# Six stages on one core: the scan's norm statistics and first front issued inside the routed stage, the second expert stage's first router front issued inside attention

## The chip, the cores and the metric

One core of one Trainium2 chip. The time is the device time of one execution in microseconds (us), the median of several runs. The core's engines work side by side from queues of their own: TensorE (PE; its weight loads are shown as PEld), VectorE (DVE), ScalarE (ACT), GpSimd (POOL), and SyncE (SP), which here issues the DMAs. Each engine takes its instructions in the order in which they are written; semaphores hold an instruction until another engine has come far enough.

## The reference

The input is 8 sequences of 512 tokens with 128 features, fp32. Six layers follow, each on a layer norm of x and added to x:

```
x = x + 0.5 * ffn0(norm(x))      # top 2 of 8 experts (128x128), softmax of the two scores
x = x + attn0(norm(x))           # attention on cos and sin features of q and k, one head
x = x + 0.5 * ffn0(norm(x))
x = x + 0.5 * ffn1(norm(x))      # 16 experts mix q, k, v and the output; causal attention
x = x + attn1(norm(x))           # selective scan: 256 channels x 16 states, convolution of 4 taps
x = x + 0.5 * ffn1(norm(x))
```

In `attn1` the normed x gives a convolved and gated u, a step dt (softplus), B and C (16 rows each) and a gate. The recurrence is `h = exp(dt*A)*h + dt*u*B`; its products with C are summed over the 16 states, `u*D` is added, the gate is applied, and a matmul leads back to 128 features.

## The kernel before

x stays in SBUF as `xs` for the whole program. The six layers run as six stages in a row, and after each stage four engines meet in a barrier (`layer_end`: drain, then a wait for all four). SyncE takes no part in it. Inside a stage the work is ordered by a clock written out by hand: each engine steps through the same slots u, issues its unit of that slot, and then the steps that `due` finds for it. A step belongs to a generator (`front(b)` prepares a sequence, `back(b)` finishes it), and a tuple of slots beside its start says when each of its pieces is issued. An engine may run ahead of the others as far as its semaphores let it.

**Expert stages (layers 0 and 2, `ffn`).** Two groups of four sequences. `front(G)` is the router of one group: VectorE's statistics of 16 tiles (L1313) and seven small operations, GpSimd's power (L566), the norm's bias on VectorE (L1328), 16 normalised tiles on ScalarE (L676), transposes on PE into bank 0 (L901), ScalarE's copies (L682), scores on PE (L909, eight matmuls a sequence), the top two on VectorE (L1331 to L1356), one exponential on ScalarE, a transpose (L933), a copy (L703). SyncE writes these rows to DRAM and reads each back over all partitions (L504, L509). Then VectorE makes one product per sequence and expert (L1397), 64 in all, and PE eight matmuls for each (L960). The front of group 0 runs before the first product; that of group 1 in the slots of group 0.

**Attention (layer 1).** Eight turns, one sequence each. `front(b+1)` (norm, q, k, v, features) is interleaved with `main(b)` (four blocks of scores, L991, exponentials, L737, weighted sum, L1000, residual on VectorE, L1433). VectorE issues norm, normalised tile and features of the next sequence, and then waits for the weighted sum. GpSimd makes only the norm's power (L571).

**Routed stages (layers 3 and 5, `routed`).** Slots of 24 a sequence: 16 expert products (L1517) with eight matmuls each for q, k and v (L1103), then 8 products for pairs of experts (L1106) that belong to the sequence before. `back(b)` is the causal attention of sequence b (L1045 to L1063 on PE, maxima L1487 on VectorE, L775 and L780 on ScalarE). The last sequence's attention has 16 slots without units around it (u = 192 to 207); its pairs come at 208 to 215, its residual (L1496) at 218.

**Scan (layer 4).** 32 slots a sequence, one of (16 states x 2 halves) each. ScalarE makes the decay (L861), GpSimd the products with B (L603) and, for five states, with C (L612); VectorE runs the recurrence (L1574) and the other products with C (L1566); PE sums over the states (L1218) and spreads C (L1206). `front(b)` makes everything that sequence b needs: on VectorE the statistics (L1260 to L1272), the bias (L1527), u (L1533), dt (L1541), gate (L1545); on ScalarE the normalised tiles (L807), copies, tanh, abs, exp and ln with three table loads; on PE transposes (L1148), convolution (L1157), the matmul for delta, B and C (L1168), two remainders (L1175), z (L1182), res (L1186). Its slots start 16 before the sequence that runs before it, so sequence 0's front stands ahead of the first recurrence, and so do the first pieces of sequence 1's. B and C go through DRAM (`bc_to_dram`, `widen_B`, `widen_C` on SyncE). The ring of products with B is six deep, that of products with C eight.

The lines that set the scan's order on VectorE before:

```
steps = on_clock(front, (-16, -14, -3, 6, 13, 16, 18, 20), back, (4, 5, 10))
for U in SCAN_CLOCK:
    if 0 <= U < ALL: scan_of(U)
    if 0 <= U - 1 < ALL and not on_pool(U - 1): times_C(U - 1)
    due(steps, U)
```

## Time and profile before

| | |
|---|---|
| median of 3 runs | 1603.86 us (1598.56 to 1604.44) |
| the profiled execution | 1601.31 us, span 1599.5 us |
| mean granted clock of TensorE | 0.935 of full speed |
| busy: PE, DVE, ACT, POOL | 1390.7, 1144.8, 529.0, 531.6 us |
| expert stage 1, attention | first product some 40 us in; attention to 271 us |
| expert stage 2 | first product 305.4 us, last residual 384.4 us |
| routed stage 1 | to 723.8 us |
| scan | first recurrence 769.0 us, last residual 1236.3 us |
| routed stage 2 | to the end |

A line in order of time has the start, the duration, the engine, the line of the code, the operation, what it writes and reads, how many instructions are merged, and in brackets how long the engine stood idle before it and what ended that. PE clocks are shares of full speed; the two levels are 1.2 and 2.4 GHz.

### The profile page before, as it was taken

The page shows a single profiled execution, that of the slowest core. Times are in us where ns is not written, and L with a number is a line of the kernel's source. Part 1 is how long each engine was busy: PE and PEld are TensorE (multiplying, and loading weights), DVE is VectorE, ACT ScalarE, POOL GpSimd, SP SyncE. Part 2 cuts the span into 40 slices and gives each one's busy share as a digit, 9 for nine tenths or more (in the row PEclk, how much of TensorE's full clock was granted, in tenths as well). Part 3 has the DMA queues.
Part 4 walks back from the last instruction along what each step waited for, and adds up shares of the span by engine and source line. Part 5 has one row for each costly group of instructions (what it writes and reads, how often), then busy time and mean ns, then how long its engine had stood idle before and what let it go on. Part 6 is the DMA issues. An engine that isn't in the chain of part 4 may idle for free.

```text
span 1599.5 us, 21272 instructions
## 1 busy us (share of the span) xinstructions
PE 1390.7 (87%) x7178; PEld 1019.3 (64%) x7178; DVE 1144.8 (72%) x2582; ACT 529.0 (33%) x1015; POOL 531.6 (33%) x446
## 2 busy tenths in 40 slices
PE   2896886599999999986988988898987689999997
PEld 2793454588899999972333333343332689999996
DVE  3786674477677777532799999999998657777753
ACT  2203443210222222214556556556542022222221
POOL 1150000000000000001798999998996000000000
PEclk9998999699999999987899999999988799999999
DMA  4560000455333333300333332332331333333330
GB/s 146 208 211 0 1 1 1 145 192 194 107 107 107 107 107 107 107 1 22 101 94 87 99 99 89 99 105 86 96 105 40 107 107 113 113 113 114 114 114 14
DMA packets 93162, 155.11 MB, mean 97 GB/s; under 512 B 11703, under 2 KB 21374, under 8 KB 92926
## 3 DMA queue, kind: packets, MB, share of 16 engines
q1 hardware_dynamic: 93054, 153.76, 30.0%
q8 instruction: 57, 0.93, 0.2%
q14 instruction: 51, 0.42, 0.1%
HBM read 150.31 MB, written 3.41 MB: 96 GB/s over the span
## 4 chain that ended last, share of the span: by engine, by line
PE 63%; DVE 15%; issue 10%; POOL 6%; ACT 3%; DMA 2%; SPq 0%; DVEq 0%; POOLq 0%; ACTq 0%
PE bank L1103 21%; PE bank L1106 7%; PE bank L1218 6%; PE bank L960 4%; POOL both L603 3%; PE bank L991 3%; PE bank L1063 2%; DVE hs L1574 2%; PE bank L1048 2%; PE bank L1115 2%; PE bank L1157 2%; PE bank L1045 2%; DVE xe L1574 2%; DVE xe L1397 2%; PE bank L1000 2%
## 5 line engine op out<-in xcount | busy, mean ns | idle before, releaser
L1103 PE MATMUL bank<-wqkv_sb,xe 128*128 128x192 f32 x2048 | 368.4, 332 | 8.2 <-DVE xe L1517 8.2
L1103 PEld LDWEIGHTS bank<-wqkv_sb,xe 128*128 128x128 f32 x2048 | 337.5, 193 | 20.0 <-DVE xe L1517 11.3
L1218 PE MATMUL bank<-both,ident 128*128 128x512 f32 x512 | 262.3, 640 | 44.6 <-DVE both L1566 44.6
L571 POOL TENSOR_TENSOR rstd<-ve,half_neg 128x4 f32<-128x4 f32 x32 | 37.9, 1184 | 728.1 <-DVE ve L1272 728.1
L861 ACT ACTIVATE bank<-dt,A 128x512 f32<-128x512 f32 x256 | 176.1, 688 | 167.5 <-DVE hs L1574 88.9
L1218 PEld LDWEIGHTS bank<-both,ident 128*128 128x128 f32 x512 | 101.8, 206 | 172.1 <-issue 104.0
L603 POOL TENSOR_TENSOR both<-du,prT 128x512 f32<-128x512 f32 x128 | 160.9, 1272 | 7.3 <-DMA prT<-bc_dram 6.8
L1574 DVE TENSOR_TENSOR_SCAN xe<-bank,both 128x512 f32<-128x512 f32 x128 | 153.7, 1209 | 11.4 <-ACT bank L861 11.4
L603 POOL TENSOR_TENSOR both<-du,prob 128x512 f32<-128x512 f32 x128 | 160.3, 1273 | 1.9 <-DVE hs L1574 1.2
L960 PE MATMUL bank<-exp_sb,xe 128*128 128x128 f32 x1024 | 130.7, 284 | 28.8 <-DVE xe L1397 28.2
L1574 DVE TENSOR_TENSOR_SCAN hs<-bank,both 128x512 f32<-128x512 f32 x128 | 153.1, 1207 | 1.2 <-ACT bank L861 1.2
L960 PEld LDWEIGHTS bank<-exp_sb,xe 128*128 128x128 f32 x1024 | 122.3, 197 | 35.5 <-DVE xe L1397 35.2
L1106 PEld LDWEIGHTS bank<-wo_sb,xe 128*128 128x128 f32 x1024 | 131.1, 193 | 4.4
L1106 PE MATMUL bank<-wo_sb,xe 128*128 128x128 f32 x1024 | 131.1, 276 | 0.0
L1517 DVE TENSOR_TENSOR xe<-at,bank 128x512 f32<-128x512 f32 x128 | 87.7, 687 | 59.1 <-PE bank L1115 59.0
L1487 DVE TENSOR_REDUCE smax<-bank 128x1 f32<-128x128 f32 (+1 forms) x64 | 31.4, 491 | 100.7 <-PE bank L1048 81.1
L1517 DVE TENSOR_TENSOR xe<-xnT,dt 128x512 f32<-128x512 f32 x128 | 85.3, 688 | 15.2 <-DMA dt<-w_rows 9.4
L780 ACT ACTIVATE prT<-bank 128x128 f32<-128x128 f32 (+1 forms) x64 | 28.0, 437 | 193.1 <-PE bank L1055 193.1
L1517 DVE TENSOR_TENSOR xe<-xnT,du 128x512 f32<-128x512 f32 x128 | 84.3, 687 | 7.6 <-PE bank L1103 6.6
L991 PE MATMUL bank<-both 128*128 128x512 f32 x128 | 63.5, 632 | 5.1 <-ACT both L730 4.7
L1157 PE MATMUL bank<-xpad,wcv 128*128 128x512 f32 x128 | 66.9, 649 | 0.0
L1566 DVE TENSOR_TENSOR both<-hs,bank 128x512 f32<-128x512 f32 x96 | 63.0, 657 | 2.2 <-issue 1.5
(256 smaller groups left out, 1978.6 us busy)
## 6 DMA issues: line engine op xcount, KB each, us to landing
dt<-w_rows SPq DMA_DIRECT2D x128, 256.0 KB, 4.1
du<-w_rows SPq DMA_DIRECT2D x128, 256.0 KB, 4.7
prob<-bc_dram SPq DMA_DIRECT2D x64, 256.0 KB, 3.3
prT<-bc_dram SPq DMA_DIRECT2D x64, 256.0 KB, 3.3
dt<-g_dram SPq DMA_DIRECT2D x32, 256.0 KB, 6.1
du<-g_dram SPq DMA_DIRECT2D x32, 256.0 KB, 6.4
g<-g_dram SPq DMA_DIRECT2D x32, 256.0 KB, 6.8
u<-g_dram SPq DMA_DIRECT2D x32, 256.0 KB, 6.7
```

The source lines that it names most:

```text
L571: pool.tensor_tensor(rstd[:], ve[:], half_neg[:, 0:NT], ALU.pow).then_inc(ln_rstd, 1)
L603: pool.tensor_tensor(dB[k % DRING], du[b % 2][:, h, :], Bs[s % RING][:], ALU.mult).then_inc(dB_made, 1)
L861: act.activation(decay[k % len(decay)][:], dt_[b % 2][:, h, :], ACT.Exp, scale=A[:, h, s:s + 1]).then_inc(dA_made, 1)
L960: m = pe.matmul(bank[7 - b % 2][:, j * P:(j + 1) * P], xe[u % RING][:, j * P:(j + 1) * P], exp_sb[:, e, :], start=(e == 0 and j == 0), sto ...
L991: m = pe.matmul(bank[2 + k % 2][:], feat[:, 2 + c, k * P:(k + 1) * P], feat[:, c, :], start=(c == 0), stop=(c == 1))
L1103: m = pe.matmul(bank[4 + j // 2][:, (j % 2) * 3 * HD:(j % 2 + 1) * 3 * HD], x_e, wqkv_sb[:, e, :], start=(e == 0 and j % 2 == 0), stop=(e ...
L1106: m = pe.matmul(bank[7][:, j * P:(j + 1) * P], x_e, wo2_sb[:, e - E2, :], start=(e == E2 and j == 0), stop=(e == UNIT - 1 and j == NT - 1))
L1157: m = pe.matmul(to, wcv[:, tap, h * P:(h + 1) * P], xpad[:, tap:tap + L], start=False, stop=(tap == 3))
L1218: pe.matmul(bank[4 + k % NH][:], ident[:], hc[k % HRING], start=False, stop=(SUM_RANK[k] == sums_of(k // UNITS, k % NH))).then_inc(hc_used, 1)
L1517: dve.tensor_tensor(xe[i % RING][:], xnT[b % 2][:] if e < E2 else at2[:], w, ALU.mult).then_inc(xe_made, 1)
L1566: dve.tensor_tensor(hc[k % HRING], hs[k % HRING][:], C_bank[d % 2][:], ALU.mult).then_inc(hc_dve, 1)
L1574: dve.tensor_tensor_scan(hs[k % HRING][:], decay[k % len(decay)][:], dB[k % DRING], 0.0, ALU.mult, ALU.add).then_inc(h_made, 1)
```

## The change

Two blocks of work are issued from another stage than before.

- The router front of group 0 of the second expert stage is a generator `ffn(2, 1, early=True)`, stepped inside attention. VectorE steps it five times in `main(4)` (statistics), once in `main(5)` (bias), and to its end in `main(7)` before it waits for the weighted sum. ScalarE makes the normalised tiles after scores 2 and 3 of turn 5 and 0 and 1 of turn 6, and copies the transposed ones after scores 2 and 3 of turn 6 and 0 and 1 of turn 7. PE transposes after scores 1, 2, 3 of turn 6 and 0 of turn 7, makes the router's scores after scores 1 and 2 of turn 7 (into bank 4), and transposes the weights before the last quarter of the last weighted sum. GpSimd's power stands before that of norm 6. Normalised tiles lie in `hs0` to `hs3`, the transposed ones of this group in `prob1`, `prT0`, `prT1` and `at2`. Semaphores of their own count them.
- The scan's statistics, up to the bias, are three new steps of the routed stage's `back(b)` at slots 54, 55 and 57 for each of the eight sequences, kept in `rstd_s` and `nmr_s`. The scan's `front` loses them on VectorE and GpSimd.
- The scan's `front(0)` is stepped inside the routed stage from slot 168 on: PE at 168 + (12, 17, 18, 19, 22, 25, 26, 28, 32, 34, 37, 39), ScalarE at 168 + (10, 14, 20, 21, 24, 27, 30, 33 to 36, 38, 41), VectorE at 168 + (22, 31, 35, 37, 39, 42). Its banks are 1 and 4 in place of 7 and 2. GpSimd makes its two products before the statistics' power of sequence 7. `front(1)` gets its own slots, which begin four slots before the first recurrence.
- SyncE writes B and C of sequence 0 before the scan's slots, and those of sequence 1 at slot 5.

The core of the diff (renamed counters of the norms are left out):

```diff
...
-def ffn_clock(front, front_at, *more):
-    return [(front(G), HALF * (G - 1), front_at) for G in range(NB // GROUP)] + list(more)
+def ffn_clock(front, first, front_at, *more):
+    return [(front(G), HALF * (G - 1), front_at) for G in range(first, NB // GROUP)] + list(more)
+def norm_at(g):
+    return g - NB * (1 if g < 2 * NB else 2 if g < 4 * NB else 3)
...
+SECOND7 = {"xT": -2, "dlt": 1, "conv0": 2, "conv1": 8, "z0": 12, "z1": 14, "res0": 16, "res1": 18}
 FRONT_IN = {"xT": 7, "dlt": 7, "conv0": 2, "conv1": 2, "z0": 2, "z1": 7, "res0": 2, "res1": 7, "out": 7}
+FIRST_IN = {7: 1, 2: 4}
...
-def on_clock(front, front_at, back=None, back_at=()):
-    return ([(back(b), UNITS * (b + 1), back_at) for b in range(NB)] if back else []) + [(front(b), UNITS * (b - 1), front_at) for b in range(NB)]
+def on_clock(front, front_at, second_at, back=None, back_at=()):
+    return ([(back(b), UNITS * (b + 1), back_at) for b in range(NB)] if back else []) + [
+        (front(b), UNITS * (b - 1), second_at if b == 1 else front_at) for b in range(1, NB)]
...
+        xn_early = [t[:].rearrange("p (j c) -> p j c", j=NT) for t in hs[0:GROUP]]
+        gxT_late = [t[:] for t in (prob[1], prT[0], prT[1], at2)] + gxT[GROUP:]
...
+                if s == 0:
+                    sp.wait_ge(at_ps, seen(NT * NB))
...
+                else:
+                    sp.wait_ge(xe_made, seen(2 * FFN + NB * UNIT))
...
             def scan():
+                bc_to_dram(0)
                 for U in SCAN_CLOCK:
-                    if (U + 4) % UNITS == 0 and 0 <= (U + 4) // UNITS + 1 < NB:
+                    if U == 5:
+                        bc_to_dram(1)
+                    if (U + 4) % UNITS == 0 and 2 <= (U + 4) // UNITS + 1 < NB:
...
+            def scan_rstd(b):
+                pool.wait_ge(sc_var, seen(b + 1))
+                pool.tensor_tensor(rstd_s[:, b, :], ve[:], half_neg[:, 0:NT], ALU.pow).then_inc(sc_rstd, 1)
             def norms(layer):
                 for b in range(1 if layer == 3 else 0, NB):
+                    if layer == 1 and b == NB - 2:
+                        group_rstd(1, 0)
                     rstd_of(layer * NB + b)
                     if layer in (3, 5):
                         invn_of((layer // 4) * NB + b)
-            def scan(layer):
+                    if layer == 3 and b >= LEAD:
+                        scan_rstd(b - LEAD)
+                if layer == 3:
+                    for b in range(NB - LEAD, NB):
+                        if b == NB - 1:
+                            finish(scan(4, early=True))
+                        scan_rstd(b)
...
-                steps = on_clock(front, (-15, 15, 18))
+                steps = on_clock(front, (15, 18), (17, 19))
...
+                        if not early:
+                            act.wait_ge(gxT_ps, seen(r * NB + GROUP * G + s - 1))
+                        to = xn_early[s] if early else xn_odd if s % 2 else xn
...
+                    ahead = GROUP if early else 2
+                    for s in range(GROUP + ahead):
+                        if s >= ahead:
+                            turned(s - ahead)
+                        if s < GROUP:
+                            normed(s)
+                        yield
...
+                group = ffn(2, 1, early=True)
                 def main(b, par, ahead):
                     act.wait_ge(acc_ps, seen(b))
@@ -736,9 +770,12 @@
                         act.wait_ge(s_ps, seen(NT * b + k + 1))
                         act.activation(PT[:, k, :], bank[2 + k % 2][:], ACT.Exp, scale=1.0 / math.sqrt(P)).then_inc(p_made, 1)
                         step(ahead, k, (0,))
+                        if 2 <= NT * (b - NB + 3) + k < 2 + 2 * GROUP:
+                            next(group)
                     finish(ahead)
                 overlapped(front, main)
+                finish(group)
...
+                if layer == 3:
+                    steps.append((scan(4, early=True), UNIT * (NB - 1), (10, 14, 20, 21, 24, 27, 30, 33, 34, 35, 36, 38, 41)))
...
+                        act.wait_ge(xe_made, seen(experts_at(0, NB - 2) + E2))
+                        act.wait_ge(bc_ps, seen(PAIRS * (NB - 1)))
+                        act.wait_ge(rows_out, 16 * NB)
...
-                steps = on_clock(front, (-13, -10, -6, -5, -2, 1, 4, 11, 12, 13, 14, 16, 19))
+                steps = on_clock(front, (-13, -10, -6, -5, -2, 1, 4, 11, 12, 13, 14, 16, 19), (-4, -1, 3, 4, 5, 7, 10, 13, 14, 15, 16, 17, 20))
...
+                        if early:
+                            pe.wait_ge(xT_sb, seen(NB))
...
+                    if early:
+                        for s in range(GROUP):
+                            turned(s)
+                            yield
+                        pe.wait_ge(turn_used, seen(2 * NB))
+                        for s in range(GROUP):
+                            scored(s)
+                            if s % 2:
+                                yield
...
+                group = ffn(2, 1, early=True)
                 def main(b, par, ahead):
                     for k in range(NT):
@@ -992,9 +1053,13 @@
                                           start=(c == 0), stop=(c == 1))
                         m.then_inc(s_ps, 1)
                         step(ahead, k, (0, 1))
+                        if 1 <= NT * (b - NB + 2) + k < 1 + GROUP + 2:
+                            next(group)
                     pe.wait_ge(acc_used, seen(layer * NB + b))
                     pe.wait_ge(v_made, seen(b + 1))
                     for k in range(NT):
+                        if b == NB - 1 and k == NT - 1:
+                            finish(group)
...
+                    steps.append((scan(4, early=True), UNIT * (NB - 1), (12, 17, 18, 19, 22, 25, 26, 28, 32, 34, 37, 39)))
...
-                steps = on_clock(front, (-11, -9, -8, -7, -4, -1, 0, 2, 9, 12, 15, 17), back, (OUT7,))
+                steps = on_clock(front, (-11, -9, -8, -7, -4, -1, 0, 2, 9, 12, 15, 17), (-2, 0, 1, 2, 4, 6, 7, 8, 12, 14, 16, 18), back, (OUT7,))
...
+                group = ffn(2, 1, early=True)
                 def main(b, par, ahead):
+                    if b == NB // 2 + 1:
+                        next(group)
                     for _ in range(3):
                         next(ahead, None)
+                    if b == NB // 2:
+                        for _ in range(5):
+                            next(group)
+                    if b == NB - 1:
+                        finish(group)
...
+                    if layer == 3:
+                        dve.wait_ge(acc_used, seen(layer * NB + b + 1))
+                        yield from moments(b, True, sc_var)
+                        yield
+                        dve.wait_ge(sc_rstd, seen(b + 1))
+                        dve.scalar_tensor_tensor(nmr_s[:, b, :], mv[:, :, 0], -1.0, rstd_s[:, b, :], ALU.mult, ALU.mult).then_inc(nmr_made, 1)
+                        yield
+                steps = by_clock(front, 1 if layer == 3 else 0, (0, 1, 3, 4, 10, 11, 12, 13, 15, 16),
+                                 back, (22, 25, 28, 31, 37, 50) + ((54, 55, 57) if layer == 3 else ()))
+                if layer == 3:
+                    steps.append((scan(4, early=True), UNIT * (NB - 1), (22, 31, 35, 37, 39, 42)))
...
-                    next(norm(g, b))
-                    yield
...
-                steps = on_clock(front, (-16, -14, -3, 6, 13, 16, 18, 20), back, (4, 5, 10))
+                steps = on_clock(front, (-3, 6, 13, 16, 18, 20), (5, 11, 15, 17, 19, 21), back, (4, 5, 10))
...
```

## Rows read from the trace of the kernel before

**Rows 1.** Order of time from attention's last residual to the expert stage's first product (start us, us, engine)
```profile
269.57 0.38 DVE L1430 RECIPROCAL rden<-bank 128x2 f32<-128x2 f32 x2 [9.84 <-PE bank L1000]
...
271.24 3.19 DVE L1313 BATCH_NORM_STATS2 gstats<-xs 128x6 f32<-128x128 f32 x16
...
275.37 0.17 DVE L1324 TENSOR_SCALAR gve<-gmv 128x16 f32<-128x16 f32 x1
...
297.95 0.28 ACT L703 ACTIVATE grows<-bank 128x128 f32<-128x128 f32 x1 [2.73 <-PE bank L933]
...
305.42 0.69 DVE L1397 TENSOR_TENSOR xe<-both,dt 128x512 f32<-128x512 f32 x1 [8.04 <-DMA dt<-g_dram]
```

**Rows 2.** Order of time from the routed stage's last residual to the first recurrence
```profile
722.64 1.13 DVE L1496 SCALAR_TENSOR_TENSOR xs<-bank,rden,xs 128x128 f32<-128x128 f32 x4 [1.92 <-PE bank L1106]
...
727.00 0.16 DVE L1527 SCALAR_TENSOR_TENSOR nmr<-mv,rstd 128x4 f32<-128x4 f32 x1 [1.21 <-POOL rstd L571]
...
769.02 2.34 DVE L1574 TENSOR_TENSOR_SCAN hs<-bank,both 128x512 f32<-128x512 f32 x2 [1.20 <-ACT bank L861]
```

**Rows 3.** Busy time by stretches, in mid-scan (stretch, length, busy us of each engine with instructions, clock, DMA)
```profile
900.00:950.00 50.00, 44.10 (x118) 18.47 (x118) 48.54 (x66) 30.75 (x48) 46.24 (x38) 0.97 0.32 91
```

**Rows 4.** Order of time, turns 5 and 6 of attention
```profile
240.56 0.38 DVE L1430 RECIPROCAL rden<-bank 128x2 f32<-128x2 f32 x2 [0.71 <-PE bank L1000]
...
243.21 1.28 ACT L737 ACT_TABLE_LOAD   x1 [2.13 <-PE bank L991]
...
246.10 1.01 PE L882 MATMUL bank<-ident,xn 128*128 128x128 f32 x4 [2.97 <-DVE xn L1277]
```

**Rows 5.** Order of time, router of the second expert stage, groups 0 and 1
```profile
291.88 0.29 DVE L1331 COPY glg<-bank 128x128 f32<-128x128 f32 x1 [13.08 <-PE bank L909]
...
297.09 0.29 DVE L1356 TENSOR_TENSOR gwts<-gwts,goh 128x128 f32<-128x128 f32 x1
...
321.44 0.96 PE L909 MATMUL bank<-gate_sb,both 128*128 128x8 f32 x8
```

**Rows 6.** A stretch of attention, and the chain of waits at three turns' first scores
```profile
175.00:180.00 5.00, 3.17 (x7) 1.83 (x8) 1.30 (x6) 1.42 (x3) 1.01 (x1) 0.66 0.00 0
...
177.98 2.71 PE bank L991 x4
...
196.00 1.73 PE bank L991 x4
...
213.04 1.73 PE bank L991 x4
```

**Rows 7.** Order of time on VectorE, a middle turn of the routed stage
```profile
549.63 0.69 DVE L1487 TENSOR_REDUCE smax<-bank 128x1 f32<-128x512 f32 x1 [3.04 <-PE bank L1048]
```

**Rows 8.** Order of time: last routed attention, and convolution matmuls of the scan's first front
```profile
696.84 0.42 DVE L1487 TENSOR_REDUCE smax<-bank 128x1 f32<-128x256 f32 x1 [2.91 <-PE bank L1048]
...
711.64 1.28 DVE L1517 TENSOR_TENSOR xe<-at,bank 128x512 f32<-128x512 f32 x2
...
741.71 3.70 PE L1157 MATMUL bank<-xpad,wcv 128*128 128x512 f32 x8
```

**Rows 9.** Groups by line and form, 726 to 756 (count, busy us, mean ns, idle before)
```profile
L807 ACT ACTIVATE xn<-xs,nmr,rstd 128x128 f32<-128x128 f32 x4 | 1.6, 482 | 16.1 <-DVE nmr L1527 16.1
...
L815 ACT ACTIVATE th<-bank 128x512 f32<-128x512 f32 x2 | 1.2, 597 | 3.4 <-PE bank L1157 3.4
```

**Rows 10.** Order of time in the scan, statistics of one sequence and of one four later
```profile
857.63 0.86 DVE L1260 BATCH_NORM_STATS2 stats<-xs 128x6 f32<-128x128 f32 x4
...
859.45 2.34 DVE L1574 TENSOR_TENSOR_SCAN hs<-bank,both 128x512 f32<-128x512 f32 x2
859.66 1.01 POOL L571 TENSOR_TENSOR rstd<-ve,half_neg 128x4 f32<-128x4 f32 x1 [4.14 <-DVE ve L1272]
...
862.29 0.85 DVE L1527 SCALAR_TENSOR_TENSOR nmr<-mv,rstd 128x4 f32<-128x4 f32 x1
...
1092.84 0.86 DVE L1260 BATCH_NORM_STATS2 stats<-xs 128x6 f32<-128x128 f32 x4
```

231 lines of the change are left out of this document (116 added, 115 removed).

## The prediction

> **What bounds the kernel now.** I read the views in this order: the busy table by stretches of 50 us, to see which engine fills each stage; the order of time around the two stage borders the diff touches; the waits by engine; and the order of time inside one turn of each stage.
>
> Two borders stand nearly empty. Attention's last residual begins behind its last weighted sum at 269.57; the router's statistics, normalised tiles, scores, top two and weight rows follow one after the other, and the expert stage's first product starts at 305.42 [rows 1]. Between routed attention's last residual (ends 723.77) and the scan's first recurrence (769.02) lie 45.3 us [rows 2]: the whole front of sequence 0, then parts of front 1. Inside the scan VectorE is busy 48.5 of 50 us, GpSimd 46.2, TensorE 44.1 at a granted clock of 0.97 [rows 3]: VectorE sets the pace, the others are close. Everything below is summed against the profiled execution (1601.3 us, span 1599.5); the median of the runs shown is 2.6 above it.
>
> **Border 1, attention to the second expert stage.** Now statistics, router and rows of group 0 run in turns 4 to 7 of attention (8 turns, counted from 0), each engine's piece at a fixed place of its queue.
> - Turn 4, VectorE: 16 statistics and seven small operations stand before its wait for the weighted sum. They took 271.24 to 275.54, 4.3 us [rows 1]. VectorE idles only 0.71 at that place of a turn [rows 4], and it then carries the path (reciprocal, residual, next norm). Cost 3.6. Between 0 and 4.3, I take the row.
> - Turn 5: one tiny operation, 0.2. ScalarE makes 8 normalised tiles (four take 1.65; mean 482 ns [rows 9]), which pushes the features of turn 6 back by about 2.1; TensorE idles 2.97 before the transposes of the next norm [rows 4], so this is hidden, with 0.9 to spare. Were it not, it costs 2.1.
> - Turn 6: TensorE gets three blocks of four transposes (0.5 each). The second and the third wait until ScalarE has copied the one before out of bank 0, and that copy stands behind the exponential of the score just made: 0.6 for either, as ScalarE's other passes over a bank [rows 9], some 0.2 of passing on, so 1.4 each. The weighted sum is queued behind them, VectorE behind that. 3 x 0.5 + 2 x 1.4 = 4.3.
> - Turn 7: transpose block with a wait of 2.5 (table load 1.28 [rows 4], exponential, copy) and 0.5; four score blocks of 0.9 (0.96 busy each [rows 5]), 3.6. Then the last quarter of the weighted sum stands behind the transposed weights. From scores copied to weights made took 291.88 to 297.38, 5.5 us [rows 5]; 4.5 us of TensorE's own work lie beside it; 1.0 stays, 0.4 for the transpose, less 0.6 that TensorE idled in the last turn before. 7.4.
> Sum: attention is 15.5 longer, its last sum ends at 285.0 and not at 269.5. The weights' rows leave at 284.1. From that copy (297.95) to the first product (305.42) took 7.5 [rows 1]: the write, the read back over all partitions, both unchanged, and SyncE stood waiting for just this. First product at 291.6 and not 305.4: **13.8 gained**. TensorE idles some 6.5 us there, before it was longer; the first matmuls stay at the low clock as before. Bounds: 8 (every wait twice my size) to 18 (the turn 6 waits fall in other idle time).
>
> **A rule that speaks against it.** The granted clock stood at 0.66 at 175 to 180, and that turn took 18.0 (177.98 to 196.00), the next one 17.0 [rows 6]. The row says that a low clock costs a turn 1 us, and that it comes with idle time of TensorE. The Trainium skill, "TensorE: Matmul & The Clock Gate" (section "A second HAM failure mode: psum-queue depth-cycling"), says that small idle times between groups of matmuls let the clock go up and down. By that rule the waits put into turns 6 and 7 bring back such turns. As a mechanism of this kernel: turns 6 and 7 at the price of the row, 1 to 2 each, some 3 in all: 1557. It counts as a rival, with 0.08; the later turns of before had 2.97 idle each and held their pace, so I don't take it.
>
> **Border 2, routed attention to scan.** Moved out of the border: sequence 0's statistics, its front on all engines, and B's and C's first broadcasts on SyncE's queue (they now precede the scan; C's first waits for the last product of the stage, which has passed).
> - Statistics of all eight sequences now follow the residuals in the routed stage: 2.0 us of VectorE in a turn of 40. At that place VectorE waited 3.04 us for scores [rows 7], and TensorE is the full one. Cost 0; uncovered it would be up to 2 x 7 = 14, which is a bound.
> - Front 0, pieces beside the last expert products and pairs (TensorE full): transposes 0.6, bias and two convolution halves 3.7 (eight such matmuls took 3.70 [rows 8], and the bias), B/C/delta matmul 0.9, first remainder 1.1: 6.2. The remainder waits for three ScalarE copies (1.9) and VectorE's gate product waits for the tanh behind those; both hold the next product of TensorE: 1.8 estimated.
> - Pieces in the latency chain of the last attention. From 696.84 (second maximum) to 711.64 (first pair product) took 14.8 at a TensorE that mostly waits [rows 8]. Another 8.5 of TensorE go in (second convolution, z, res, remainder). Before, TensorE ran slow there; walking its queue at full clock, the new matmuls mostly fall into the waits for maxima and exponentials, and the last of the attended rows comes 0.8 earlier than before. But ScalarE now has table load, absolute value and exponential ahead of their copy, 1.8 more than it waited: +1.0 net.
> - Then VectorE's first pair product stands behind the first gate g, which waits for ScalarE: ln 0.6, abs and exp 1.2, ln 0.6, tanh 0.6 [rows 9], table load 1.28 [rows 4], and g 0.7 on VectorE itself: 5.1, in place of 0.45: +4.7.
> - After the last residual: statistics of sequence 7 up to its bias, as before for sequence 0 (723.77 to 727.16, 3.4 [rows 2]); then border, ScalarE's four normalised tiles of front 1 (1.65) and the first decay (0.7): 2.6 with the passing on. So 6.0 where 45.3 stood.
> 45.3 - 6.0 - 6.2 - 1.8 - 1.0 - 4.7 = **25.6 gained**. Bounds: 12 (front at half clock: 8 more; routed statistics half uncovered: 7) to 33 (the chain hides all of its 8.5 and the clock rises with the work).
>
> **Inside the scan.** Statistics of sequences 2 to 7 leave VectorE's queue. One took 857.63 to 859.45, 1.8, and its bias 0.85 [rows 10], of which 0.8 keeps the next instruction back: 2.6 in each of six periods of 58.8 (857.63 to 1092.84 are four [rows 10]), 15.6 in all. GpSimd loses its 1.0 operation and the 4.1 that it waited for it [rows 10]; TensorE's hole of the same place goes. What is late next: GpSimd has 44 products a period at 46.24/38 = 1.22 [rows 3], 53.5; TensorE 44.1/50 of 58.8, 51.9. VectorE's new period is 56.2, so it stays the bound, barely; I take 12 of the 15.6. Against that front 1 now lies whole in the first period: 0.7 of VectorE, 3 of ScalarE, 7 of TensorE partly at the low clock: 2 lost (bounds 0 and 7, all of TensorE's). **10 gained**, bounds -4 and 15.6.
>
> **Sum.** 13.8 + 25.6 + 10 = 49.4; against the profiled 1601.3 that is 1551.9, on the median's footing 1554.5. Forecast 1554.
>
> **Rivals.**
> - A, the scan keeps its pace: GpSimd or TensorE takes over at once when the statistics go. For: both over 88% busy. Against: GpSimd waited 4.1 at each statistics, so it runs ahead. The 12 go: 1566.
> - B, the tail of the routed stage costs more: a queue held in order, or the low clock there. For: three engines wait for one another at fixed places, TensorE was slow there before. Border 2 gives only 12: 1568.
> - C, the clock rule above: 1557.
> - D, slower than before: with its holes elsewhere, TensorE gets the low clock in much of the scan and becomes its bound. It needs 51.9 x 0.97 = 50.3 us a period at full clock. The first 39 gained at the borders and 10 less are eaten when a period is 58.8 + 39.4/8 = 63.7, so at a mean granted clock of 0.79. At 0.70 a period is 71.9, 8 x 13.1 = 105 longer: 1603.9 - 39.4 + 105 = 1669. Against: the clock was 0.97 [rows 3] and idle time shrinks.
> - E, border 1 gives nothing, since the first product waits for something other than the rows: 13.8 lost and 15.5 paid: 1583. Against: SyncE waited for the copy alone.
>
> **How the numbers follow.** Forecast 0.64, A 0.12, B 0.10, C 0.08, D 0.02, E 0.02; 0.02 for anything else that leaves it no faster. The forecast's bounds together reach from 1538 to 1588; ends that add up are rare. 1541 to 1577 leaves out D, E and the tails, 2 in 10. About 0.5% is what a measurement of this kernel can tell from no change (its three runs span 0.4%); faster 0.95, within 0.5% 0.02, slower 0.03.
>
> **What would show it.** Right: first expert product some 7 us behind the copy of the weights and 5 behind the last attention residual; turn 4 at 20.6, turn 6 at 21.3; the routed stage some 14 longer to its last residual; first recurrence 6 us behind that; scan periods of 56 to 57 with VectorE still at 97%. Wrong: periods of 58 (A); a routed turn above 41 before the last one, or TensorE at half clock through the tail (B); a granted clock below 0.8 in the scan (D).

## The result and the profile after

The changed kernel took 1558.55 us (median of four executions, 1555.88 to 1562.80) beside 1601.23 for the kernel before: ratio 0.974, 95% interval 0.972 to 0.976, so 2.6% faster. The forecast was 1554, its range 1541 to 1577. A later set of six executions of the same kernel gave 1552.06 to 1571.85, median 1570.47, ratio 0.980 (0.976 to 0.983). The times of one kernel thus lie up to 20 us apart. The experiments explain the larger part of that; the rest stays open.

The profiled execution took 1555.88 (span 1554.1). I split the two spans at events that both have; columns in us. The rows leave out 1.0 between the expert stage's last residual and the first routed product, the same in both:

| stretch | before | after | gain | forecast |
|---|---|---|---|---|
| start to turn 2's reciprocal (same code) | 189.46 | 188.14 | 1.3 | 0 |
| from there to the first expert product | 115.96 | 105.03 | 10.9 | 13.8 |
| to the expert stage's last residual (its second half is the same code) | 78.27 | 79.54 | -1.3 | 0 |
| first routed product to last routed residual | 337.96 | 353.94 | -16.0 | -13.7 |
| last routed residual to first recurrence | 46.38 | 6.72 | 39.7 | 39.3 |
| first recurrence to last scan residual | 466.57 | 456.03 | 10.5 | 10 |
| rest | 363.91 | 363.71 | 0.2 | 0 |

45.4 came of 49.4. The first two blocks of rows are the order of time at border 1, turns 4 to 7 (start us, us, engine, line, out<-in, count, idle before and its releaser). They answer to [rows 1, 4 and 5].
```profile
205.18 0.37 DVE L1520 RECIPROCAL rden<-bank 128x2 f32<-128x2 f32 x2 [0.71 <-PE bank L1065]
...
221.43 3.18 DVE L1391 BATCH_NORM_STATS2 gstats<-xs 128x6 f32<-128x128 f32 x16
...
222.91 1.88 PE L1052 MATMUL bank<-both 128*128 128x512 f32 x4
...
225.64 0.37 DVE L1520 RECIPROCAL rden<-bank 128x2 f32<-128x2 f32 x2
...
225.81 2.90 POOL L589 TENSOR_TENSOR grstd<-gve,half_neg 128x16 f32<-128x16 f32 x1 [15.62 <-DVE gve L1402]
...
228.74 0.18 DVE L1406 SCALAR_TENSOR_TENSOR gnmr<-gmv,grstd 128x16 f32<-128x16 f32 x1 [0.98 <-POOL grstd L589]
...
232.33 1.15 PE L927 MATMUL bank<-ident,xn 128*128 128x128 f32 x4 [7.54 <-DVE xn L1355]
```
```profile
233.28 3.62 PE L1052 MATMUL bank<-both 128*128 128x512 f32 x4
...
245.74 0.37 DVE L1520 RECIPROCAL rden<-bank 128x2 f32<-128x2 f32 x2 [0.71 <-PE bank L1065]
...
266.89 0.38 DVE L1520 RECIPROCAL rden<-bank 128x2 f32<-128x2 f32 x2 [4.82 <-PE bank L1065]
...
271.98 0.66 PE L947 MATMUL bank<-ident,hs 128*128 128x128 f32 x4 [2.52 <-ACT prT L718]
...
285.50 0.28 ACT L732 ACTIVATE grows<-bank 128x128 f32<-128x128 f32 x1 [2.58 <-PE bank L989]
...
286.39 0.38 DVE L1520 RECIPROCAL rden<-bank 128x2 f32<-128x2 f32 x2 [1.32 <-PE bank L1065]
...
293.17 0.69 DVE L1478 TENSOR_TENSOR xe<-prob,dt 128x512 f32<-128x512 f32 x1 [5.25 <-DMA dt<-g_dram]
```
The reciprocals mark the turns: turn 4 is 205.18 to 225.64, 20.5; then 20.1, 21.1 and 19.5, where before had 17.0 three times and 12.0. Turn 5 is the surprise. VectorE waits 0.98 for GpSimd's power (16 values in each partition). TensorE has a hole, a time with nothing to do, of 7.54 (2.97 in [rows 4]): 3.4 of the 4.6 more are the statistics that stand ahead of the reciprocal of turn 4, 1.2 the wait for GpSimd. The four instructions of score products behind that hole take 3.62; the four ahead of it took 1.88. (An fp32 product of the program is two instructions in these rows.) The busy time by stretches shows the clock there (stretch, length, busy us of PE, PEld, DVE, ACT, POOL, granted clock, DMA share, GB/s): 0.51, the lower level (1.2 GHz).
```profile
225.00:230.00 5.00, 0.00 (x0) 0.00 (x0) 3.82 (x20) 1.75 (x2) 2.90 (x1) 1.00 0.00 0
230.00:235.00 5.00, 2.67 (x7) 1.51 (x8) 1.73 (x9) 0.60 (x1) 1.01 (x1) 0.51 0.00 0
```
The routed stage's end and border 2, in order of time again; the rows answer to [rows 2 and 8]:
```profile
695.09 0.42 DVE L1577 TENSOR_REDUCE smax<-bank 128x1 f32<-128x256 f32 x1 [2.35 <-PE bank L1113]
...
698.68 3.78 PE L1226 MATMUL bank<-xpad,wcv 128*128 128x512 f32 x4
...
702.68 2.81 PE L1226 MATMUL bank<-xpad,wcv 128*128 128x512 f32 x4
...
705.86 0.49 ACT L817 ACTIVATE prT<-bank 128x384 f32<-128x384 f32 x1 [6.15 <-PE bank L1120]
...
712.79 0.58 ACT L820 ACTIVATE at<-bank 128x512 f32<-128x512 f32 x1
...
718.24 1.92 DVE L1617 TENSOR_TENSOR xe<-at,bank 128x512 f32<-128x512 f32 x3
...
727.64 1.12 DVE L1586 SCALAR_TENSOR_TENSOR xs<-bank,rden,xs 128x128 f32<-128x128 f32 x4 [1.93 <-PE bank L1171]
...
734.36 2.34 DVE L1671 TENSOR_TENSOR_SCAN hs<-bank,both 128x512 f32<-128x512 f32 x2 [2.40 <-ACT bank L906]
```
The first recurrence stands 5.6 behind the residual's end, forecast 6.0. From second maximum (695.09) to first pair product (718.24) it is 23.2, forecast 14.8 + 1.0 + 4.7 = 20.5: the eight instructions of the convolution's second half ran mostly at the lower level, 6.6 in place of 3.7. No experiment takes border 2 alone back; its account rests on this split and on the scan-filled kernel below, where that convolution ran at full clock.

### The profile page after: what moved, and what is told of

Read it like the earlier page. It is cut to its first block, busy times and chain, and to the rows that moved or that the text cites. A ratio compares the mean times of both kernels' runs of the same rounds, so it can differ in the third digit from the quotient of the medians.

```text
span 1554.1 us, 21262 instructions
## 1 busy us (share of the span) xinstructions
PE 1371.8 (88%) x7178; PEld 1009.1 (65%) x7178; DVE 1139.7 (73%) x2582; ACT 526.5 (34%) x1015; POOL 532.6 (34%) x446
## 4 chain that ended last, share of the span: by engine, by line
PE 68%; DVE 14%; issue 10%; ACT 3%; POOL 2%; DMA 1%; SPq 0%; DVEq 0%; POOLq 0%; ACTq 0%
PE bank L1168 22%; PE bank L1292 8%; PE bank L1171 7%; PE bank L1019 5%; PE bank L1226 3%; PE bank L1052 2%; PE bank L1128 2%; PE bank L1113 2%; DVE hs L1671 2%; DVE xe L1671 2%; PE bank L1110 2%; DVE xe L1478 2%; PE bank L1180 2%; DVE both L1663 1%; PE bank L1120 1%
## 5 line engine op out<-in xcount | busy, mean ns | idle before, releaser
L1168 PEld LDWEIGHTS bank<-wqkv_sb,xe 128*128 128x128 f32 x2048 | 339.1, 194 | 18.7 <-DVE xe L1617 10.2
L1292 PE MATMUL bank<-both,ident 128*128 128x512 f32 x512 | 254.4, 623 | 27.7 <-DVE both L1663 27.6
L594 POOL TENSOR_TENSOR rstd<-ve,half_neg 128x4 f32<-128x4 f32 x24 | 29.8, 1243 | 577.8 <-DVE ve L1346 577.8
L1671 DVE TENSOR_TENSOR_SCAN xe<-bank,both 128x512 f32<-128x512 f32 x128 | 153.9, 1211 | 11.8 <-ACT bank L906 11.8
```

The source lines that it names most:

```text
L1168: m = pe.matmul(bank[4 + j // 2][:, (j % 2) * 3 * HD:(j % 2 + 1) * 3 * HD], x_e, wqkv_sb[:, e, :], start=(e == 0 and j % 2 == 0), stop=(e ...
L1292: pe.matmul(bank[4 + k % NH][:], ident[:], hc[k % HRING], start=False, stop=(SUM_RANK[k] == sums_of(k // UNITS, k % NH))).then_inc(hc_used, 1)
L1671: dve.tensor_tensor_scan(hs[k % HRING][:], decay[k % len(decay)][:], dB[k % DRING], 0.0, ALU.mult, ALU.add).then_inc(h_made, 1)
```

## The experiments

All medians stand beside the kernel before on the same chip (1600.1, 1598.6 and 1598.7 in the three sets). The code cuts are extracts.

**Border 1 put back.** The early router front is taken out of attention, the rest stays:
```
-                    for G in range(1 if layer == 2 else 0, NB // GROUP):
+                    for G in range(NB // GROUP):
-                        if 1 <= NT * (b - NB + 2) + k < 1 + GROUP + 2:
-                            next(group)
```


> The changed kernel with border 1 put back: the second expert stage makes its first router front itself, as before; everything at border 2 and in the scan stays changed. Theory (the traces' sums): border 1 gave 10.9 us net (12.25 at the first product less the 1.3 that the turns ahead of it already differed), so 1567, about 11 above the changed kernel, with the turns 4 to 6 back at 17.0 us and a granted clock of 1.00 in them. Rival (border 1 gave nothing, the first product waits for something else, what was saved came from elsewhere): 1556, no change. Rival (the gain of border 2 hangs on the earlier start, over the clock's phase): more than 3 us away from 1567 either way.

Median 1571.6 (1562.0 to 1582.6), ratio 0.983 (0.979 to 0.987). In its profile the turns are 17.04 again, and from turn 2's reciprocal to the first expert product it is 115.85, against 105.03 in the changed kernel and 115.96 before: border 1 gives 10.8, as its term of the table says, and the rival of no gain falls. But its span, 1575.5, is 21.4 above the changed kernel's, not 11: its scan, whose code is the same, took 466.5 where the changed one had 456.0, and its routed stage 356.3 against 353.9. The median is 4.6 above the expected 1567, which was the sign of the third rival (border 2 hangs on the earlier start). The repeat of the changed kernel below gives the same long scan with border 1 in place, so that rival isn't needed. This was the first sign of a second pace.

**Statistics of sequences 2 to 7 back in the scan.**
```
+                    if b >= 2:
+                        yield from moments(b, False, sc_var)
+                        yield
+                        dve.wait_ge(sc_rstd, seen(b + 1))
+                        dve.scalar_tensor_tensor(nmr_s[:, b, :], ...).then_inc(nmr_made, 1)
+                        yield
```


> The changed kernel with the statistics of sequences 2 to 7 put back into the scan, on VectorE and GpSimd, where they stood before; only those of sequences 0 and 1 are made in the routed stage. Theory (they cost the scan 1.8 + 0.8 us of VectorE in each of six periods, and cost nothing in the routed stage): the scan periods go from 56.5 to 58.5 us, the routed stage stays at 355, the whole 10 to 15 longer, 1568. Rival (the scan's gain came from TensorE's higher granted clock, 0.97 against 0.93 in later periods, and not from the statistics): 3 or less longer, 1559. Rival (the statistics also cost the routed stage's end): it gets 1 to 2 shorter, and the whole only 8 longer.

Median 1569.87 (1566.8 to 1572.1), ratio 0.982 (0.980 to 0.984). The middle periods are 58.3 to 59.9 (58.5 was expected), and 3.2 came back at border 2, where sequence 7's statistics no longer stand. Against the changed kernel's first set the median is 11 longer, against its second set nothing. Inconclusive alone: the two causes need to be parted.

**TensorE's hole in turn 5 filled.**
```
+                    if b == 6:
+                        pe.wait_ge(xT_sb, seen(ln_at(g)))
+                        for _ in range(7):
+                            pe.matmul(bank[0][:], ident[:], exp_sb[:, 0:NT, :]..., start=True, stop=True)
                     xT(g)
```


> The changed kernel with seven products of no use (identity by weights, 128x512, into the bank that the next transposes overwrite) ahead of the transposes of turn 5 of attention, where TensorE idled 7.54 us. Output unchanged. Theory (it is this hole that lets the granted clock fall to 0.51, and the low clock made the four score products behind it take 3.62 instead of 1.88 and the projections more): the clock stays at 1.00, turn 5 goes from 20.1 to 18.2 us, the rest of its excess being VectorE's wait for GpSimd; 1.5 to 2 shorter, 1554. Rival (the low clock is not from the hole): turn 5 stays at 20.1 and the clock falls all the same; no change. Should the products outlast the hole, the transposes come late by at most 0.5.

Turn 5 took 18.20 (expected 18.2), with these rows (the products of no use, then the score products behind the transposes):
```profile
226.97 6.17 PE L1035 MATMUL bank<-exp_sb,ident 128*128 128x512 f32 x14
234.68 1.01 PE L927 MATMUL bank<-ident,xn 128*128 128x128 f32 x4 [1.53 <-DVE xn L1359]
235.52 1.89 PE L1056 MATMUL bank<-both 128*128 128x512 f32 x4
```
The granted clock is 1.00 there, and the turn is 1.9 shorter than the 19.9 to 20.1 of every profile with the hole: the low clock cost that much of the 3.1 that turn 5 lost, and the rest is the wait for GpSimd. But nothing was won. In this profile the clock fell two turns later, behind a wait of 2.51: it was 0.66 at 273 to 278, four instructions of scores took 3.39, and turn 7 took 21.19, where the changed kernel had 19.50 at 1.00 behind the same wait (2.52). From turn 2's reciprocal to the first expert product it is 104.91, against 105.03. The whole, 1562.64 (1553.7 to 1566.4), ratio 0.977 (0.974 to 0.979), could not resolve 2 us in any case: the scan of this profile took 466.1.

**The group's statistics spread over turns 1 to 4**, behind the normalised tiles:
```
-                    if b == NB // 2 + 1:
-                        next(group)
-                    for _ in range(3):
-                        next(ahead, None)
-                    if b == NB // 2:
-                        for _ in range(5):
-                            next(group)
+                    for i in range(3):
+                        next(ahead, None)
+                        if i == 1 and 1 <= b <= GROUP + 1:
+                            next(group)
+                        if i == 1 and b == GROUP:
+                            next(group)
```


> The changed kernel with the group statistics taken out of the place before turn 4's reciprocal: one sequence's four statistics in each of the turns 1 to 4, the seven small operations in turn 4 and the bias in turn 5, each between the normalised tiles and the wait for the projections, where VectorE idles 3.0 us a turn. Theory (the hold-up of VectorE there, then GpSimd's 2.9 us in its path and TensorE's hole with its low clock are one cause): turns 4 and 5 go back from 20.5 and 20.1 to 17.0 and 17.0, 6.5 us less, 1549 to 1550. Rival (the hole of 3.0 us is itself on the path, since the next features follow): turns 1 to 4 lengthen by 0.9, 0.9, 0.9 and 1.9, and 2 us are left. Rival (GpSimd's operation stays in the path through its queue): turn 5 still 1 to 3 longer.

Turns 4 and 5 took 17.04 each, and turn 2's reciprocal to first product 98.55 (105.03): 6.5, as expected. VectorE's wait for the projections, 3.0 in each turn, is free room; the place ahead of the reciprocal wasn't. Yet the median is 1561.93, ratio 0.974 (0.970 to 0.978), not the expected 1549 to 1550, with executions from 1544.9 to 1564.5; the profiled one had a scan of 466.8.

**The changed kernel once more**, unedited.

> The changed kernel once more, nothing edited, to see how often it gives which scan. So far its scan took 456 us (periods of 55.8 and 56.8, granted clock 0.97) in one profile, while the same scan code took 466 (periods of 58.0, clock 0.93) in three profiles of other experiments. Theory (one kernel, two paces of the scan, which it is depends on how TensorE's clock falls and rises in each period): its times fall into two groups some 6 to 10 us apart, around 1556 and 1563. Rival (the other kernels differ in something of their own): all its times lie within 1556 to 1562 and the scan takes 456.

1552.06, 1566.03 and four of 1570.4 to 1571.9, so not the two groups at 1556 and 1563 that were expected. The profiled one (1570.56) had a scan of 466.19 with middle periods of 57.7 to 58.0: one kernel, two paces of the scan. Between the two profiled executions lie 14.7 us; 10.2 are the scan, 1.6 the routed stage ahead of it, and 2.6 the code behind it, where the last turn took 25.9 and 22.6. Two periods show where the paces part; order of time, this execution:
```profile
1007.08 1.12 PE L1292 MATMUL bank<-both,ident 128*128 128x512 f32 x2 [2.33 <-DVE both L1663]
1009.39 1.11 PE L1217 MATMUL bank<-ident,xn 128*128 128x128 f32 x4 [1.19 <-DVE g L1639]
1010.29 6.01 PE L1292 MATMUL bank<-both,ident 128*128 128x512 f32 x8
...
1016.62 0.69 DVE L1663 TENSOR_TENSOR both<-hs,bank 128x512 f32<-128x512 f32 x1 [0.50 <-DVE hs L1671]
...
1020.51 0.59 ACT L864 ACTIVATE wT<-bank 32x512 bf16<-32x512 f32 x1 [3.66 <-PE bank L1239]
...
1020.78 0.69 DVE L1663 TENSOR_TENSOR both<-hs,bank 128x512 f32<-128x512 f32 x1 [0.63 <-DVE hs L1671]
...
1022.93 1.23 DVE L1671 TENSOR_TENSOR_SCAN xe<-bank,both 128x512 f32<-128x512 f32 x1 [1.46 <-ACT bank L906]
```
The same place in the first profile of the changed kernel:
```profile
1055.81 1.81 PE L1292 MATMUL bank<-both,ident 128*128 128x512 f32 x2 [2.33 <-DVE both L1663]
1058.13 1.12 PE L1217 MATMUL bank<-ident,xn 128*128 128x128 f32 x4 [0.51 <-DVE g L1639]
1059.03 3.85 PE L1292 MATMUL bank<-both,ident 128*128 128x512 f32 x8
...
1067.09 0.59 ACT L864 ACTIVATE wT<-bank 32x512 bf16<-32x512 f32 x1 [1.50 <-PE bank L1239]
```
Once a period TensorE has little to do (it waits for a product of VectorE and for bank 7, held until VectorE has made the second gate), and its clock falls. What differs is when. In the first profile one sum (two instructions) in the middle of the hole took 1.81, and the eight instructions of sums behind it 3.85. In this one the sum in the middle took 1.12 and the eight behind it 6.01. TensorE is then late with the product that ScalarE copies (it waits 3.66 for it, against 1.50), the decays behind that copy come late, and VectorE itself waits, 2.6 in its three rows. (Two of the three waits are put down to VectorE's own `hs`. By the times it was the spread C: TensorE's products for it, L1280, end 0.1 before either.)

**The scan's hole filled.**
```
                             sum_of(k)
+                    if U % UNITS in (19, 20, 21) and 0 <= U < ALL - UNITS:
+                        pe.wait_ge(g_made, seen(NH * (U // UNITS + 1) + 1))
+                        pe.matmul(bank[2][:], ident[:], wcv[:, 0:2, :]..., start=True, stop=True)
```


> The changed kernel with three products of no use (identity by convolution weights, 128x512) in each of the first seven scan periods, at slots 19, 20 and 21, where TensorE has little to do: into bank 2, which is free from the gate of res0 to the next convolution. Output unchanged. Theory (in that place the clock falls to 0.5, eight sums behind it take 3.9 to 6.0 us, and VectorE then waits up to 2.6 us for what TensorE owes it): the clock stays at 1.00 through the periods, all periods are 55 to 56, the scan takes 450 to 456 in every run, 1548 to 1556, and the two groups of times are gone. Rival (TensorE has no room: it is busy 46 of 50): the products add up to 2.8 us a period, the scan takes 466 to 480. Rival (the pace is VectorE's alone, whatever the clock): 456 or 466, as without.

1550.98, ratio 0.970 (0.969 to 0.972), and its four executions lie within 1.2 us (1550.54 to 1551.73). That narrow a spread did not come again: the kernels below with the same filled scan have 4.9 to 9.5. Five periods are 55.15 to the hundredth. The order of time at the hole, now:
```profile
990.88 1.98 PE L1306 MATMUL bank<-wcv,ident 128*128 128x512 f32 x4 [0.62 <-DVE g L1642]
...
993.56 1.02 PE L1306 MATMUL bank<-wcv,ident 128*128 128x512 f32 x2
...
994.91 0.66 PE L1217 MATMUL bank<-ident,xn 128*128 128x128 f32 x4 [0.32 <-DVE g L1642]
995.40 3.60 PE L1292 MATMUL bank<-both,ident 128*128 128x512 f32 x8
```
And the stretch 900 to 950 (columns as above), of the changed kernel's first profile, of its second, and of this one:
```profile
900.00:950.00 50.00, 45.94 (x121) 19.17 (x120) 48.27 (x57) 31.17 (x49) 47.41 (x40) 0.97 0.34 101
```
```profile
900.00:950.00 50.00, 46.46 (x123) 19.07 (x121) 46.86 (x55) 30.43 (x48) 46.44 (x39) 1.00 0.30 92
```
```profile
900.00:950.00 50.00, 47.85 (x130) 20.30 (x128) 49.32 (x58) 30.98 (x49) 48.93 (x40) 1.00 0.32 98
```
VectorE goes from 48.27 or 46.86 to 49.32 of 50. Over the five middle periods its work is the same in all three, 54.5 to 54.7 a period; its idle time is 1.7, 3.2 and now 0.7. Only here does VectorE's own work set nearly all of the pace. The middle row also warns that one stretch's clock tells little: it is 1.00 because the dip of its period fell into the next one, 950 to 1000, where it is 0.93. More work on TensorE, 3 us a period by its rows, made each middle period 0.7 to 2.9 shorter.

**Filled, with the statistics back in the scan.** Both edits above.

> The scan-filled kernel with the statistics of sequences 2 to 7 back in the scan. With TensorE's clock held up its difference to the scan-filled one is the price of the statistics alone. Theory (my term: 2.6 us of VectorE in each of six periods, less what is given back): periods of 57.2 to 58.2, the scan 10 to 14 longer than scan-filled, and some 4 of it returned at the routed stage's end; 1558 to 1565. Rival (VectorE had room, and the gain of the changed kernel's scan came from the clock): within 4 of scan-filled.

1563.95, ratio 0.979 (0.977 to 0.981). Periods of 58.03 to 58.08 against 55.15, scan 468.9 against 450.8; border 2 gives back 3.2, and the whole is 13.0 longer. That is the price of the statistics in the scan, 2.9 a period (forecast 2.6 of queue, 12 taken): VectorE's work is 56.9 a period instead of 54.5, so 2.4 are work and 0.5 more idle time. TensorE's clock was not wholly held up here, 0.97 over these periods against 1.00, so part of the 0.5 may be the clock's. In the routed stage the statistics cost nothing: 351.3 us without those of sequences 2 to 7, 351.2 with them.

**The kernel before, filled.**

> The kernel before with the same three products in its scan periods, nothing else changed. Theory (VectorE set its pace but lost 1 to 2 us a period to the low clock as well: 2.0 idle at 1049 to 1057): periods of 57.2 to 58 in place of 58.2 to 59.8, 5 to 9 us less, 1591 to 1595. Rival (VectorE's pace does not depend on the clock there): within 2 of before. Rival (the hole of 4.9 us before bank 2 comes free is what drops the clock, and three products behind it do not hold it): no change either, with the clock still at 0.5 for some us a period.

1595.36 (1594.2 to 1599.4), ratio 0.9985 (0.9975 to 0.9996): 3.3 us, less than the 5 to 9 expected. Periods of 57.8 to 58.0 for 58.2 to 59.8. The dip of the clock was there before the change and cost about 1 us a period. My reading, which no run tests, is that the statistics on VectorE gave TensorE the time to catch up, and the change took that time away.

**Border 1 mended twice, scan filled.** The spread statistics, and transposes between the quarters of turn 6's weighted sum with their copies on VectorE:
```
+                    if b == NB - 2:
+                        for s in range(GROUP):
+                            dve.wait_ge(gxT_ps, seen(NB + s + 1))
+                            dve.tensor_copy(gxT_late[s], bank[0][:]).then_inc(gxT_sb, 1)
```


> The scan-filled kernel (1551.0), so that the scan's two paces don't blur it, with border 1 mended twice: the spread statistics of the earlier experiment, and the four transpose blocks all in turn 6 (one before and three between the four quarters of the weighted sum), their copies out of bank 0 on VectorE, which waited 4.82 us there, in place of ScalarE. Theory (turn 6's excess is transposes 2.0 and waits for ScalarE's copies, behind its exponentials; turn 7's is one more such wait of 2.5): turns 4 and 5 at 17.0, turn 6 at 19.0 to 19.3 (not 21.15), turn 7 at 16.5 (not 19.5), 11.6 less in all, 1539 to 1541. Rival (turn 6's waits are for ScalarE's exponentials themselves, which remain): turn 6 stays near 21, only turn 7 gains; 1542 to 1544.

1542.40 (1538.8 to 1547.6), ratio 0.965 (0.962 to 0.968): 8.6 less than scan-filled, not 11.6. Turn 7 gave more than expected (15.02), turn 6 nothing (21.46, at a granted clock of 1.00). The first copy stands behind VectorE's features, and TensorE waits 2.23 for it. The kernel with both mends, below, has the same edit and the same wait; there the clock fell behind it too (0.66 at 255 to 260), and turn 6 took 22.91. Its rows:
```profile
251.50 0.60 PE L947 MATMUL bank<-ident,hs 128*128 128x128 f32 x4
...
254.48 0.68 DVE L1533 COPY prob<-bank 128x512 f32<-128x512 f32 x1
...
255.22 0.66 PE L947 MATMUL bank<-ident,hs 128*128 128x128 f32 x4 [2.23 <-DVE prob L1533]
```
The rival's numbers came (turn 6 near 21, 1542 to 1544), but it had named the wrong engine, ScalarE; the theory overlooked VectorE's queue.

Turn 5 of this profile, meant to take 17.0, took 19.60:
```profile
227.54 1.16 PE L927 MATMUL bank<-ident,xn 128*128 128x128 f32 x4 [2.97 <-DVE xn L1360]
228.48 3.62 PE L1052 MATMUL bank<-both 128*128 128x512 f32 x4
```
The hole is the 2.97 of every turn, which in the turns ahead of it and in the kernel with both mends left the clock at 1.00 and the turn at 17.0. Here the clock was 0.56 at 226 to 231. So the longer hole of the changed kernel isn't needed for a fall; the usual one can bring it as well, in one execution and not in another.

**The routed stage's end mended, scan filled.** Banks of its own for front 0, the second convolution half early, dt and gates late:
```
-FIRST_IN = {7: 1, 2: 4}
+FIRST = {"xT": 1, "dlt": 1, "conv0": 4, "conv1": 5, "z0": 4, "z1": 1, "res0": 5, "res1": 6}
-                    steps.append((scan(4, early=True), UNIT * (NB - 1), (22, 31, 35, 37, 39, 42)))
+                    steps.append((scan(4, early=True), UNIT * (NB - 1), (22, 31, 41, 43, 45, 47)))
```


> The scan-filled kernel with the end of the routed stage mended: conv1, res0 and res1 of front 0 in banks of their own (5, 5 and 6), the convolution's second half beside the pair products of the turn before, not inside the latency chain of the last attention; logarithms, table loads, both dt and both g behind the first pair products instead of ahead of them. Theory (the 23.2 us from second maximum to first pair product hold 6.6 for conv1 at half clock, in ScalarE's and VectorE's way, and 4.9 from the attended copy to the first pair product): that stretch goes to 15 to 17, the turn ahead of it is 2 to 4 longer; 4 to 7 less, 1544 to 1547. Rival (what leaves the chain only turns waits for maxima and exponentials visible, at half clock): 2 or less.

1547.75 (1543.0 to 1549.9), ratio 0.967 (0.965 to 0.970): 3.2 less. In the profiles second maximum to first pair product is 17.0 (697.83 to 714.82) against 19.9 in scan-filled's, the last residual comes 5.0 sooner behind the one before, but that turn before is 3.0 longer: 2.0 net, the rival's figure, where the theory had 4 to 7. With its work gone from the chain TensorE runs there at the lower level:
```profile
700.00:705.00 5.00, 3.99 (x13) 2.21 (x13) 2.37 (x13) 2.23 (x5) 1.01 (x1) 0.59 0.00 0
705.00:710.00 5.00, 5.00 (x18) 3.78 (x17) 1.51 (x4) 1.38 (x3) 0.00 (x0) 0.50 0.00 0
```

**Both mends.**

> Both of these in one kernel. Theory (the two borders are separate terms): the sum of both gains, 15 to 19 below scan-filled, 1532 to 1536, and 4% below the kernel before. Rival (they share the clock's state and do not add): 1540.

1538.68 (1532.5 to 1540.9), ratio 0.962 (0.959 to 0.964). The gains of the two, 8.6 and 3.2, add to 11.8; 12.3 was measured. They add, as the theory had it, but its sum of 15 to 19 rested on the two forecasts that had missed. This version beats both kernels: 3.8% below the one before, and 1.3 to 1.8% below the changed one (0.962 beside its 0.974 and 0.980, from other sets).

**More products of no use.**

> The kernel with both mends and more products of no use: six at the start of the second expert stage (while the weights' rows travel, TensorE idles 6 us and then multiplies at half clock), four at the end of the routed stage, and one in every second slot of the last scan period and a third of the one before. Theory (the low clock costs at each of these: 1 to 1.5 at the expert stage's start, 1 to 2 in the first scan period, 1.5 in the last, where 41.4 stands against 39.9): 3 to 5 less than without, 1528 to 1532. Rival (these places wait for DMA, VectorE and GpSimd, not for TensorE): no change, or 1 longer for the products in the way.

1540.18 (1538.5 to 1543.4), ratio 0.963 (0.962 to 0.965): no gain, the rival's outcome. The mean granted clock is 0.966, the highest of all, against 0.961; yet the expert stage took 78.65 in both, the first scan period 78.96 and 79.03, and the last two together 95.6 and 96.0. Over the first 5 us of the expert stage the granted clock was 1.00 with them and 0.59 without, for the same 78.65: TensorE's clock is not what that stage waits for there.

## Why the prediction was right, and where it was not

- **Border 1, forecast 13.8, got 10.9** (10.8 by the first experiment). Turn 4 (forecast 3.6, got 3.4), turn 6 (4.3, 4.1), turn 7 (7.4, 7.5) and the way of the rows (7.5, 7.7) held. The step that failed is "Turn 5: one tiny operation, 0.2": it took 3.1. The tiny operation waits for GpSimd's power, and TensorE lost the clock in a hole that the hold-up of VectorE in turn 4 had lengthened. The filled hole parts the two, 1.9 for the clock and 1.2 for the wait; spreading the statistics removed both. The price of rival C's rule, "turns 6 and 7 at the price of the row, 1 to 2 each", appeared one turn earlier, and in turn 7 of the filled-hole profile (1.7). The argument against C, that holes of 2.97 had held their pace, doesn't carry: in the kernel with border 1 mended twice such a hole lost the clock and 2.6 us. For its place the Trainium skill, "TensorE: Matmul & The Clock Gate" (section "A second HAM failure mode: psum-queue depth-cycling"), speaks of small idle times; the changed kernel's trace shows one of 7.5, that of the kernel with border 1 mended twice one of 2.97.
- **Border 2, forecast 25.6, got 23.7.** Residual to recurrence and the pieces beside the expert products were right (7.6 for that turn, forecast 8.0). 1.6 of the stage's extra 16.0 lies in its first turn, whose code is unchanged: after a DMA wait the granted clock is 0.70 at 408 to 413, where before had 1.00 at the same distance into the stage (419 to 424). The rest is the convolution inside the chain at half clock, "mostly fall into the waits" as the prediction put it. In scan-filled's profile, with the clock at 1.00 from 695 to 710 and in that first turn, the stage took 351.2: 13.2 longer, against a forecast of 13.7. (The prediction's pieces add to 6.3 and 5.0 where it writes 6.2 and 5.1; the two cancel.)
- **The scan, forecast 10, got 10.5, partly by luck.** The term of the statistics was, if anything, too small: 18.2 in the scan, by the pair of filled kernels. What I took off it stands for something else than I thought. The prediction asked whether GpSimd or TensorE "takes over at once" over whole periods, by mean busy times, 51.9 against 56.2; neither does. TensorE takes over for a few microseconds in each period, behind its dip, and takes back 0.7 to 2.9 of the 2.9. The forecast saw the low clock only as rival D, all or nothing ("a mean granted clock of 0.79"), at 0.02. Its mild form is what happens: at 0.94 over the middle periods all of the scan's gain goes, as rival A would have it, and the four executions near 1571 are 5 above A's 1566. Of the five profiles with this scan unfilled one has 456.0 and four have 466.1 to 466.8, with A's sign, periods of 58: the forecast of 10 was met by the one profile of the faster pace, and that was luck.
- The range held every execution of either set. With the dips of the scan filled the changed kernel is 47.6 below the kernel before, of the 49.4 summed; but 3.3 of that the same filling gives the kernel before, and filled against filled the change gives 44.4.

What stays open: which of the two paces an execution gets, and what else spreads the times. The routed stage ahead of the scan took 349.7 to 356.3 in the seven profiles in which its code is the same, and its low clock comes and goes between them as in attention (granted clock 0.54 at 700 to 705 in the changed kernel's first profile, 1.00 in scan-filled's). No run here shows what decides it.

## What to carry to other kernels

When work is taken off the engine that sets the pace, the next engine must be looked at where it is worst, not in its mean: list its holes inside one period, and what stands right behind them. A hole in TensorE's work can cost twice, and the second time it is paid by whoever waits for the products behind it. A few products of no use into a free bank lowered the time where they stood in a hole that came back in every period of the scan. In attention they shortened one turn and the clock fell in another, and in places where TensorE's clock wasn't waited for they brought nothing. A gain of 2 us in a kernel whose executions lie up to 20 apart has to be read in the trace, over a stretch that holds the later turns too. A step moved into another stage goes where its engine already waits for something (3.0 us in each turn here), and its wait for a third engine is placed a turn later than its issue.

## What the runs showed of the hardware

- TensorE's lower level follows its holes (7.54 us in attention; 2.33 and 0.51, or 2.33 and 1.19, with one sum between in the scan), and when it comes differs between executions: eight instructions of the sums behind the same hole took 3.85 and 6.01 us, and 3.60 with the hole filled.
- The same hole can bring it or not: behind 2.97 us the granted clock was 0.56 in one execution (turn of 19.6) and 1.00 in others (17.0); behind 2.5 us it was 0.66 in one (21.2) and 1.00 in another (19.5).
- Part of the spread of a kernel's times came from its own holes: the scan took 456.0 or 466.2 us in two profiles of one kernel, and 450.3 to 450.8 in the profiles of all five kernels with its holes filled and the statistics out of it.
- GpSimd's power took 2.90 us on 128x16 values, and 1.01 on 128x4 in attention (1.39 in the routed stage).
